# Per-batch layout of the scan's DRAM tensors, an earlier and serial folding step, `pull` ahead of the reduce, and attention key copies shared between two engines

## The reference, cut to what matters

```python
# layer 0, token mixer (state: 16 x 16 per batch and head)
def step(state, rkv):
    r_t, k_t, v_t = rkv
    pred = jnp.einsum('bhij,bhj->bhi', state, k_t)
    err = pred - v_t
    state = dec * state - et * (err[..., :, None] * k_t[..., None, :])
    n = jnp.maximum(jnp.sqrt(jnp.sum(state * state, axis=(-2, -1), keepdims=True)), 1e-08)
    state = state * jnp.where(n > max_norm, max_norm / n, 1.0)
    wkv = jnp.einsum('bhij,bhj->bhi', state, r_t)
    return (state, wkv)
# layers 0 and 1, cross-attention with 16 heads (layer 0 causal)
scores = jnp.einsum('bthd,bshd->bhts', Q, K) / jnp.sqrt(jnp.float32(DH))
P = jax.nn.softmax(scores, axis=-1)
out = jnp.einsum('bhts,bshd->bthd', P, V).reshape(B, Tq, D) @ Wo + b_o
```

## Time and profile before

| | us |
|---|---|
| median of 3 runs | 6573.78 (6573.76 to 6576.15) |
| profiled execution, its own time | 6573.78 |
| its span in the trace | 6572.0 |

### The profile page before, as it was taken

One profiled execution on the slowest core, in us unless ns is written; L12 is line 12 of the kernel. 1 busy time (PEld: TensorE's weight loads), 2 busy tenths in 40 slices (PEclk: granted clock), 3 DMA queues, 4 the chain that ended last, 5 costly groups with the idle time before them and its releaser, 6 DMA issues. The chain is left out here.

```text
span 6572.0 us, 178792 instructions
## 1 busy us (share of the span) xinstructions
PE 5933.9 (90%) x76324; PEld 4297.4 (65%) x76324; DVE 5402.7 (82%) x10662; ACT 3611.6 (55%) x8176; POOL 3730.2 (57%) x1761
## 2 busy tenths in 40 slices
PE   7677776999989899999999999999788799999999
PEld 5577765777767655555555555555566478888888
DVE  7899995555558799999999999999566588888886
ACT  5555553444424587888888787877465422222221
POOL 1688883111101399999999999999322122222222
PEclk9788887999989999999999999999899999999999
DMA  3332221111014401120211111120221100000000
GB/s 98 94 91 63 63 52 55 35 49 52 22 47 149 126 26 47 46 60 28 64 44 42 41 45 47 38 60 15 66 86 53 45 7 9 9 8 9 8 9 7
DMA packets 383703, 314.53 MB, mean 48 GB/s; under 512 B 164534, under 2 KB 351673, under 8 KB 382396
## 3 DMA queue, kind: packets, MB, share of 16 engines
q1 hardware_dynamic: 377334, 302.81, 15.8%
q10 hardware_dynamic: 5574, 0.29, 0.1%
HBM read 194.99 MB, written 108.01 MB: 46 GB/s over the span
## 5 line engine op out<-in xcount | busy, mean ns | idle before, releaser
L2385 POOL TENSOR_TENSOR ss_ch<-ss_h,ss_c_all 128x2048 f32<-128x2048 f32 x511 | 2325.5, 4612 | 33.5 <-DVE ss_h L2414 22.8
L2414 DVE TENSOR_TENSOR_SCAN ss_h<-ss_decay,banks 128x1024 f32<-128x1024 f32 x1024 | 2256.4, 2266 | 63.7 <-PE banks L2301 63.1
L2301 PE MATMUL banks<-ss_diag,ss_dxT 128*32 128x256 f32 x32768 | 1969.6, 381 | 26.4 <-DVE ss_h L2414 17.5
L2301 PEld LDWEIGHTS banks<-ss_diag,ss_dxT 128*32 128x32 f32 x32768 | 1008.9, 110 | 807.0 <-DVE ss_h L2414 196.5
L2365 ACT ACTIVATE ss_decay<-ss_dt,ss_neg_a 128x510 f32<-128x510 f32 x2048 | 1358.3, 710 | 257.3 <-DVE ss_h L2414 250.9
L2752 POOL TENSOR_TENSOR pk_blockhot<-pk_onehot,pk_parts 128x2048 bf16<-128x2048 bf16 x96 | 345.5, 3626 | 921.1 <-DVE pk_parts L2978 921.1
L2356 ACT ACTIVATE ss_diag<-ident,ss_bT 128x128 f32<-128x128 f32 x2016 | 685.5, 387 | 184.4 <-PE banks L2301 184.4
L2308 PE MATMUL banks<-ss_ch,ss_stacked 128*32 128x256 f32 x8192 | 635.5, 382 | 45.2 <-POOL ss_ch L2385 40.3
L821 PE MATMUL banks<-ms_rprod,ident 128*128 128x128 f32 x2048 | 463.8, 399 | 204.8 <-POOL ms_rprod L946 204.8
L821 PEld LDWEIGHTS banks<-ms_rprod,ident 128*128 128x128 f32 x2048 | 429.3, 250 | 232.9 <-POOL ms_rprod L946 182.4
L1061 POOL TENSOR_SCALAR l_ln_mv<-l_ln_mv 128x2 f32<-128x2 f32 x64 | 15.0, 234 | 961.7 <-DVE l_ln_mv L1056 961.7
(11 more groups left out here) (328 smaller groups left out, 9926.8 us busy)
## 6 DMA issues: line engine op xcount, KB each, us to landing
ss_dt<-keep_dt SPq DMA_DIRECT2D x256, 128.0 KB, 4.0
ss_c_all<-keep_cn SPq DMA_DIRECT2D x512, 64.0 KB, 2.0
keep_v<-ms_cx_values SPq DMA_DIRECT2D x32, 512.0 KB, 3.0
l_va<-keep_v SPq DMA_DIRECT2D x32, 512.0 KB, 4.5
l_kf<-keep_k SPq DMA_DIRECT2D x32, 256.0 KB, 3.4
keep_x<-l_x SPq DMA_DIRECT2D x32, 256.0 KB, 2.2
keep_xc<-si_xc SPq DMA_DIRECT2D x16, 512.0 KB, 3.8
keep_zs<-si_zs SPq DMA_DIRECT2D x16, 512.0 KB, 4.7
```

The source lines that it names most:

```text
L2301: m = T_.matmul(inp[u % 2][s * CB:(s + 1) * CB, g, :, t * P:(t + 1) * P], inputs[i % 2][0][:, g, t, u * CB:(u + 1) * CB], diag[slot][:, g, ...
L2385: G_.tensor_tensor(ch[u // 2 % 4][:, :, :, :, :].rearrange("p j g n t -> p j (g n t)"), h[u // 2 % 4][:, :, :, :, :].rearrange("p j g n t ...
L2414: V.tensor_tensor_scan(whole(h[u // 2 % 4][:, u % 2, :, :, :]), whole(decay[u % 4]), whole(inp[u % 2]), 0.0, ALU.mult, ALU.add).then_inc(s ...
```

## The change

1. **Layout.** The DRAM tensors r, k, v and wkv are (B, T, C) in place of (T, B, C). In `mixer_scan` each chunk load of k, v or r becomes 16 DMAs, one for each sequence (8 partitions each), and so does each wkv store; the semaphores count 16 times as much. Stores and loads of the neighbouring stages only change their address.
2. **Folding.** PE multiplies in front of u = 1 and at once waits for ACT's copy; ACT copies in front of u = 3. SP no longer loads the next piece early: store and next load stand together at the end of the chunk, behind the wkv store.
3. **Step.** L995 (`pull`) comes ahead of L993 (reduce), and L997 waits for the last of both.
4. **Attention.** For pairs 0, 2, 4 and 6 VectorE copies the turned keys to `kT` (`turns_vector`), ACT only for the odd pairs. In `layer0_rest` the new program stands last in VectorE's round, in `layer1_attention` second, behind the maxima.

```diff
 class Folding:
-    def load(self, S, c):
+    def sync(self, S, c):
         done, coming = self.piece(c), self.piece(c + 1)
         if done is not None:
-            S.wait_ge(*self.folded.at(done))
+            S.wait_ge(*self.copied.at(done))
+            S.dma_start(self.wk_out[:, done * NH * NK:(done + 1) * NH * NK], self.wk[:, :]).then_inc(self.stored.sem, DMA)
         if coming is not None:
...
             S.dma_start(self.keys[:, :, :], self.io["keysT"][:, heads, :]).then_inc(self.loaded.sem, DMA)
...
         m.then_inc(self.folded.sem, 1)
-
-    def taken(self, T_, c):
-        n = self.piece(c)
-        if n is not None:
-            T_.wait_ge(*self.copied.at(n))
+        T_.wait_ge(*self.copied.at(n))
...
 def mixer_scan(chip):
-        of_chunk = dst[:, c % RING, :, :, :] if name == "r" else dst[:, tokens(c), :, :]
-        engine.dma_start(of_chunk.rearrange("p t e d -> p t (e d)"), by_heads(name, c)).then_inc(steps[c % 2].sem, DMA)
+        for b in range(B):
+            of_chunk = dst[:, c % RING, :, :, :] if name == "r" else dst[:, tokens(c), :, :]
+            engine.dma_start(of_chunk[b * HP:(b + 1) * HP, :, :, :].rearrange("h t e d -> h t (e d)"),
+                             dr[name][b][tokens(c)].rearrange("t (h x) -> h t x", h=HP)).then_inc(steps[c % 2].sem, DMA)
...
-            folding.load(S, c)
             for _ in work:
                 pass
             if c:
                 store(S, c - 1)
             if c == 2:
                 rest.load(S)
-            folding.store(S, c)
+            folding.sync(S, c)
...
-        S.dma_start(by_heads("wkv", c), WKV[:, c % 2, :, :, :].rearrange("p t e d -> p t (e d)")).then_inc(stored[c % 2].sem, DMA)
+        for b in range(B):
+            ps = slice(b * HP, (b + 1) * HP)
+            S.dma_start(dr["wkv"][b][tokens(c)].rearrange("t (h x) -> h t x", h=HP),
+                        WKV[ps, c % 2, :, :, :].rearrange("h t e d -> h t (e d)")).then_inc(stored[c % 2].sem, DMA)
...
-            if t % CH == FOLD:
+            if t % CH == 1:
                 folding.tensor(T_, t // CH, context)
             if t % CH == LATE:
-                folding.taken(T_, t // CH)
                 work = context.tensor(T_, t // CH)
...
-            if t % CH == FOLD + 2:
+            if t % CH == 3:
                 folding.scalar(A, t // CH)
...
         if t:
+            V.tensor_tensor(pull[:, :, :], err, rep(gain[:, t, :], 2, D), ALU.mult).then_inc(*own.up())
             if t > 1:
                 V.wait_ge(*multiplied.at(t - 2))
                 V.tensor_reduce(ahead, kprod[t % 2][:, :, :, :], AX.X, ALU.add).then_inc(*own.up())
-            looked = own.now()
-            V.tensor_tensor(pull[:, :, :], err, rep(gain[:, t, :], 2, D), ALU.mult).then_inc(*own.up())
-            V.wait_ge(*looked)
+            V.wait_ge(*own.now())
             V.tensor_tensor(raw, ahead, rep(fdec[:, :], 2, D), ALU.mult).then_inc(*own.up())
...
 class Attention:
-            T_.wait_ge(*self.kT_copied.at(b, pair + 1))
+            T_.wait_ge(*(self.kT_copied if pair % 2 else self.kT_copied_v).at(b, pair // 2 + 1))
             self.heads_down(T_, self.qps[b % self.splits], 2 * pair).then_inc(self.q_turned.sem, 1)
...
+    def turns_vector(self, V, b):
+        for pair in range(8):
+            if pair % 2 == 0:
+                V.wait_ge(*self.k_turned.at(b, pair + 1))
+                V.tensor_copy(self.pair_of(self.kT[b % 2], pair), self.bank[self.TURN][:, :]).then_inc(self.kT_copied_v.sem, 1)
+            yield
+            yield
...
     def turns_scalar(self, A, b):
         for pair in range(8):
-            A.wait_ge(*self.k_turned.at(b, pair + 1))
-            A.copy(self.pair_of(self.kT[b % 2], pair), self.bank[self.TURN][:, :]).then_inc(self.kT_copied.sem, 1)
+            if pair % 2:
+                A.wait_ge(*self.k_turned.at(b, pair + 1))
+                A.copy(self.pair_of(self.kT[b % 2], pair), self.bank[self.TURN][:, :]).then_inc(self.kT_copied.sem, 1)
...
 def layer0_rest(chip, entry):
             if n + 2 < B:
                 now.append(enter_vector(V, n + 2))
+            if 0 <= n + 1 < B:
+                now.append(at.turns_vector(V, n + 1))
             rounds(now)
...
 def layer1_attention(chip, entry):
         at.flow([(at.maxima_vector(V, b), b, at.MAXIMA) for b in range(B)]
+                + [(at.turns_vector(V, b), b, at.TURNS) for b in range(B)]
                 + [(at.finish_vector(V, b, x_ready), b, at.PROJECTED - 3) for b in range(B)]
...
 def build(nc, io):
-    dr = {n: dram(n, (B, T, C)) for n in ("g", "x1", "x2", "x3")}
-    dr |= {n: dram(n, (T, B, C)) for n in ("r", "k", "v", "wkv")}
+    dr = {n: dram(n, (B, T, C)) for n in ("r", "k", "v", "g", "wkv", "x1", "x2", "x3")}
```

More of the change, by code:

```diff
@@ L333, in sync @@
         for n, c in enumerate(NAMES):
-            S.dma_start(rows(dr[c][b] if c == "g" else dr[c][:, b, :]), z.res[:, n, :, :]).then_inc(z.stored.sem, DMA)
+            S.dma_start(rows(dr[c][b]), z.res[:, n, :, :]).then_inc(z.stored.sem, DMA)
         yield
@@ L608, in load @@
             S.dma_start(self.keys[:, :, :], self.io["keysT"][:, heads, :]).then_inc(self.loaded.sem, DMA)
[L610 to L614, removed]
     def tensor(self, T_, c, context):
@@ L726, in mixer_scan @@
     HP, CH, GR = H // 2, 16, 4
-    CHUNKS, LATE, FOLD = T // CH, 5, 2
+    CHUNKS, LATE = T // CH, 5
     RATE, GAIN = (8, 9), (9, 10, 11, 12)
@@ L751, in mixer_scan @@
     rates, sigmoids = st.mark("rates_loaded", 2 * DMA), st.mark("sigmoids", 2)
-    steps = [st.mark(f"steps_loaded{n}", 3 * DMA) for n in range(2)]
+    steps = [st.mark(f"steps_loaded{n}", 3 * B * DMA) for n in range(2)]
     own, eks, gains_made = st.steps("vector"), st.mark("ek_ready", 2), st.mark("gains_multiplied", CH // GR)
@@ L757, in mixer_scan @@
     measured, spread_root, spread_ready = st.mark("measured"), st.mark("spread_root"), st.mark("spread_ready")
-    norm_spread, norm_ready, stored = st.mark("norm_spread"), st.mark("norm_ready"), [st.mark(f"wkv_stored{n}", DMA) for n in range(2)]
+    norm_spread, norm_ready, stored = st.mark("norm_spread"), st.mark("norm_ready"), [st.mark(f"wkv_stored{n}", B * DMA) for n in range(2)]
     def tokens(c):
         return slice(c * CH, (c + 1) * CH)
-    def by_heads(name, c):
-        return dr[name][tokens(c)].rearrange("t b c -> t (b c)").rearrange("t (p x) -> p t x", p=P)
     def load_steps(engine, c, name, dst):
@@ L1101, in __init__ @@
         self.k_own, self.own, self.q_own = st.steps("k_own"), st.steps("vector"), st.steps("q_own")
-        self.k_split, self.k_turned, self.kT_copied = mark("k_split"), mark("k_turned", 8), mark("kT_copied", 8)
+        self.k_split, self.k_turned, self.kT_copied, self.kT_copied_v = mark("k_split"), mark("k_turned", 8), mark("kT_copied", 4), mark("kT_copied_v", 4)
         self.h1_turned, self.hT1_ready, self.q_projected, self.q_biased = mark("h1_turned"), mark("hT1_ready"), mark("q_projected"), mark("q_biased")
@@ L1455, in turns_tensor, with turns_vector @@
                 T_.wait_ge(*self.q_repeated.at(b))
-            T_.wait_ge(*self.kT_copied.at(b, pair + 1))
+            T_.wait_ge(*(self.kT_copied if pair % 2 else self.kT_copied_v).at(b, pair // 2 + 1))
             self.heads_down(T_, qp, 2 * pair).then_inc(self.q_turned.sem, 1)
+            yield
+    def turns_vector(self, V, b):
+        for pair in range(8):
+            if pair % 2 == 0:
+                if b > 1:
+                    V.wait_ge(*self.rescored.at(b - 2, 2 * pair + 2))
+                V.wait_ge(*self.k_turned.at(b, pair + 1))
+                V.tensor_copy(self.pair_of(self.kT[b % 2], pair), self.bank[self.TURN][:, :]).then_inc(self.kT_copied_v.sem, 1)
+            yield
             yield
@@ L1676, in load @@
                 S.wait_ge(*mixed.at(b - 2))
-            S.dma_start(wkv[b % 2][:, :, :], rows(dr["wkv"][:, b, :])).then_inc(wkv_loaded[b % 2].sem, DMA)
+            S.dma_start(wkv[b % 2][:, :, :], rows(dr["wkv"][b])).then_inc(wkv_loaded[b % 2].sem, DMA)
             S.dma_start(gate[b % 2][:, :, :], rows(dr["g"][b])).then_inc(wkv_loaded[b % 2].sem, DMA)
```

## The result

The changed kernel takes 6643.36 us (median of 4 runs, 6637.04 to 6645.38) against 6573.77, 70 us more; 85 were forecast. Over all 25 executions on record its median is 6640.84, 67 us more, and the ratio is 1.0100, 95% interval 1.0089 to 1.0112. The profiled execution has a span of 6642.2 us, 70.2 more than before. Where they arise is read from the same event in each trace.

A forecast was written before the change was run, and what follows sets the result against it. VectorE was taken to bound the recurrence and PE layer 0's attention, with nothing full in layer 1's. Step 29, head 9, tail 4, folding 7, layer 0 27 and layer 1 9 sum to 85 on 6573.8: 6659 us, range 6618 to 6706.

The forecast's parts named there:

- The step: Recurrence, 254 steps: `pull` ahead of the reduce delays VectorE's own chain by 0.115 us each, +29 us (20 to 46).
- The order of two operations: Recurrence step: by the skill's rule the order of `pull` and reduce would not matter, making the 29 us term nought.
- The head: Start of the recurrence: SP's 32 small transfers of k and v land later, +9 us (5 to 14).
- the tail: End of the recurrence: sixteen wkv store issues and a landing delay the next stage, +4 us (2 to 6.5).
- The middle: Recurrence between its ends: SP's small loads, about 31 us per 50 us chunk, stay hidden by VectorE's steps.
- Folding: Folding in the recurrence: keys issued behind 16 wkv stores arrive late, ScalarE idles, VectorE waits, +7 us (0 to 20).
- Layer 0: Layer 0's attention: VectorE's key copies stand last in the round and delay PE in pairs 2, 4, 6, +27 us (13 to 41).
- Layer 1: Layer 1's attention, pair 4's round: a copy between two VectorE reduces adds 0.6 us, 15 times, +9 us (0 to 19).
- (a): Rival, recurrence step: the reorder is free, by the skill's rule or the root wait swallowing it, 6630 us; chance 0.10.
- (b): Rival, recurrence: SP or the DMA engines become the bound, from 0.72 us per small transfer, 6680 to 6860 us; chance 0.09.
- (c): Rival, attention: not slower, as ScalarE's relief shortens the rounds by more than the rest costs, 6565 us; chance 0.04.

The follow-up runs named there:

- The first experiment: The kernel before with only the step's order changed, `pull` ahead of the reduce: 6593.94 against 6577.68 us, ratio 1.0024.

## Why the prediction was right, and what of it was not

Every part had the sign and the place that was forecast: 70 us against 85, inside the range. The parts alone add up, in time to 16.3 + 29.2 + 23.7 + 3.8 = 73.0, each with an interval of 6 to 9 us to either side, and in stage lengths to 17.7 + 24.9 + 23.2 + 4.4 = 70.2. That the sum came within 15 us is luck in part: step, head, tail and both attentions were too large by 22 us together, and folding was too small by 6.

- **The step, +29, measured +17.** The direction was right. The step of the working that failed is the sentence that the root is not what sets this step. It was argued from L1004, which starts 0.11 after the root's end, but the root's reader is L1001, which starts 0.03 after it, and from there the way goes through the reciprocal to L1011. The root ended last by about 0.05, so the first 0.05 of a delay of 0.10 on VectorE's own chain hid behind it. The value 0.115 for the slot was also a little high; the runs say 0.10. 164 plain steps × 0.05 + 90 steps with work beside the root × 0.10 = 17.2, and 17.7 was measured. The lower bound of 20 was above the truth, as it was made from the slot alone and not from what the slot could hide behind.
- **The order of two operations.** The Trainium skill ("VectorE: DVE Perf Modes", section "The DRAIN you can't avoid"), read as the prediction read it, would have made the order free. The first experiment says +16 us: the rows were the better guide. The same section also says that an operation that isn't held starts earlier, and this is what the trace shows: `pull` runs in the end of the reduce when it stands behind it, and pushes the reduce by 0.10 when it stands ahead.
- **The head, +9, measured +6.9, and the tail, +4, measured +2.8.** The mechanism was right. I took 0.43 us per issue from transfers of 64 KB; those of 8 partitions have a median of 0.32 and come every 0.38.
- **The middle.** Hidden, as forecast: body +0.6 with the layout alone. The Trainium skill ("DMA: Bandwidth & Descriptors", section "Rules for kernel authors") says that such transfers stay on at most as many engines as their outermost dimension has, 8 here. No run here shows on how many they ran, and whatever it was did not bind.
- **Folding, +7, measured +13.4.** The chain was right, link by link; the term was mis-sized because each link was taken too short. With the first piece, from the end of the last context store to the issue of the keys I had 7.3 us, it was 7.6; from there to PE's start 4.3, it was 5.4; PE's product 1.91, it was 2.60. The four products took 2.60, 2.61, 2.30 and 3.68 us. ScalarE waited for them 4.1, 4.3, 3.7 and 5.1 us, 17.1 in sum, in place of my 1.2 + 3 × 2.5 = 8.7. The share of it that reached VectorE, 13.4 of 17.1, is near the one I took, 7 of 8.7. What the prediction did not say is that neither edit has this cost alone: folding's order by itself costs nothing, and the layout costs nothing in the middle.
- **Layer 0, +27, measured +24.** Each pair came as forecast, and with 14 sequences they make 14 × 2.06 = 28.8 us, as in the sum before my discount (29). The stage grew by less, 23.2 alone and 24.7 in the changed kernel. Some 2 us of that come back in pair 3, whose query turn follows its key turn after 1.06 in place of 1.21 us; the rest is no larger than the stage's scatter.
- **Layer 1, +9, measured +4.** The place was right, PE waits 6.4 us longer for the maxima. What failed is the overlap: I took nothing off the 15 × 0.6, and 7.0 us went out of another wait of PE in the same stage, the one for `l_h`.
- **The rivals.** (a), the order free: no, but its second reason, that the wait on the root swallows the reorder, was half right, with 0.05 of 0.10 in each plain step, some 8 us. (b), SP the bound: no, 0.38 against the deciding 0.72. (c), ScalarE's relief helps: no, no attention stage became shorter.

No version tried that computes everything beats the kernel before. The closest to the changed kernel that is better than it has folding's loads ahead of the small stores.

## What to carry to other kernels

Before an instruction is called off the path, ask of each of its inputs who reads it and when that reader was free. Where two chains end within 0.1 us of each other, as here, a delay on the earlier one costs only what the later one doesn't cover: 0.05 of 0.10. Splitting a transfer cost nothing where a chunk of lead hid it (+0.6 us), but it lengthens the queue for whatever is issued behind it: here a load behind sixteen small stores, in four places, cost 13.4 us. A copy moved to an engine that looks idle costs above all its place in that engine's order: here 1.37 us for an instruction of 0.68, and 0.11 where only the longer duration counted.

## What the runs showed of the hardware

A folding piece's product is the same 16 matmuls everywhere. It took 1.91 us in all twelve cases in which its data lay ready (the kernel before, folding's order alone, folding's loads ahead). In all eight in which PE had waited 1.9 to 2.8 us for it, it took longer: 2.60, 2.61, 2.30 and 3.68 us in the changed kernel, 2.05, 3.68, 3.17 and 2.97 with layout and folding together. Windows of the kernel after, in the waiting stretch of the first piece, in its product and behind it (length, busy PE, PEld, DVE, ACT, POOL, granted clock, DMA share, GB/s), then the product of the kernel with folding's loads ahead:

```profile
438.50:441.00 2.50, 0.00 (x0) 0.00 (x0) 2.43 (x13) 0.64 (x3) 1.94 (x2) 1.00 0.90 267
441.00:443.70 2.70, 2.60 (x16) 2.41 (x16) 1.18 (x4) 0.00 (x0) 2.50 (x2) 0.74 0.29 45
443.70:446.00 2.30, 1.63 (x7) 1.63 (x8) 0.58 (x5) 1.81 (x8) 0.00 (x0) 0.50 0.30 46
```

```profile
439.70:441.80 2.10, 2.10 (x18) 1.96 (x16) 2.03 (x10) 0.96 (x5) 2.10 (x2) 1.00 0.61 161
```

PE did nothing for 2.6 us, and the granted clock then fell within the product: 0.74 over it and 0.50 behind it, which is 1.2 of 2.4 GHz. The product's matmuls went from 0.275 to 0.42 us each from the eleventh on; in the fourth piece all of them were slow. So with the waits for data went another 3.6 us in the four products of the changed kernel. Whether the wait is what lowers the clock there was not tried.
